# Where down's return is added in a fused attention and feed-forward kernel: one addition, one load and three subtractions change their places

## The reference, cut to what matters

```python
def attn(x):                                   # x: [16, 512, 256]
    qkv = relu(einsum('bnc,oc->bno', x, qkv_weight)).reshape(B, N, 3, 32, 8)
    q, k, v = qkv[:, :, 0], qkv[:, :, 1], qkv[:, :, 2]
    v_pad = concatenate([v, ones], axis=-1)
    vk = einsum('bnhe,bnhd->bhed', v_pad, k)
    vk_q = einsum('bhed,bnhd->bnhe', vk, q)
    att = vk_q[..., :8] / (vk_q[..., 8:] + 1e-15)
    return einsum('bnc,oc->bno', att.reshape(B, N, 256), proj_weight) + proj_bias

def ffn(x):                                    # weights are int / 127, hidden size 768
    return einsum('bsh,dh->bsd', silu(x @ wg.T) * (x @ wu.T), wd)

x1  = layernorm(x + attn(x))
out = layernorm(x1 + ffn(x1))
```

## Time and profile before

| | |
|---|---|
| time, median of 3 runs | 508.27 us (506.55 to 509.43) |
| time of the profiled execution | 506.2 us, its span 504.2 us |
| granted clock of TensorE | 0.998 over the span |
| busy: TensorE, its weight load, VectorE, ScalarE, GpSimd | 486.4, 404.4, 415.6, 255.1, 85.3 us (TensorE 96% of the span) |
| chain that ended last, by engine | TensorE 39%, DMA 24%, VectorE 22%, issue 9% |
| DMA | 85.29 MB, mean 169 GB/s |

### The profile page before, as it was taken

How to read it: one execution, slowest core, us unless ns; L and a number is a source line. 1 busy time by engine, 2 the same in 40 slices (tenths; PEclk the granted TensorE clock), 3 DMA queues, 4 the chain that set the end, 5 groups by cost and what they waited for, 6 DMA issues and landing times.

```text
span 504.2 us, 11235 instructions
## 1 busy us (share of the span) xinstructions
PE 486.4 (96%) x4292; PEld 404.4 (80%) x4292; DVE 415.6 (82%) x939; ACT 255.1 (51%) x441; POOL 85.3 (17%) x94
## 2 busy tenths in 40 slices
PE   8999999989999999999999999999999999899996
PEld 5888887868878788888887878788887887789885
DVE  5878778769879697897969879697896969799896
ACT  4667344455445444545554446444445454355553
POOL 1330110302103021020302103021030302113011
PEclk9999999999999999999999999999999999999999
DMA  8325174283763828457383763928457382632212
GB/s 327 143 76 168 42 230 148 86 282 110 249 191 133 272 94 275 141 202 229 109 273 102 253 205 111 292 96 276 140 201 221 110 280 64 223 128 72 85 42 86
DMA packets 67368, 85.29 MB, mean 169 GB/s; under 512 B 3984, under 2 KB 46736, under 8 KB 67344
## 3 DMA queue, kind: packets, MB, share of 16 engines
q1 hardware_dynamic: 67200, 84.70, 50.7%
q10 hardware_dynamic: 144, 0.26, 0.2%
HBM read 48.24 MB, written 36.18 MB: 167 GB/s over the span
## 4 chain that ended last, share of the span: by engine, by line
PE 39%; DMA 24%; DVE 22%; issue 9%; POOL 2%; ACT 2%; SPq 1%; POOLq 0%; DVEq 0%; ACTq 0%
PE abcd_ps L1050 17%; DMA down_way<-qT_first 12%; PE up_ps L1050 11%; DMA wqp_raw<-down_way 7%; PE gate_ps L1050 5%; DVE h L612 4%; PE abcd_ps L1102 3%; DVE h_lo L605 3%; DVE st L681 2%; DVE x1T_lo L605 2%; DVE xT_lo L605 2%; DMA wd_raw<-x_way 2%; DMA x_way<-wu_raw 2%; PE gate_ps L1080 2%; DVE r L698 1%
## 5 line engine op out<-in xcount | busy, mean ns | idle before, releaser
L408 ACT ACTIVATE h_hi<-h 128x512 fp32r<-128x512 f32 (+1 forms) x97 | 60.7, 627 | 92.9 <-DVE h L612 92.2
L330 POOL TENSOR_TENSOR rstd<-ve,minus_half 128x4 f32<-128x4 f32 (+2 forms) x36 | 35.2, 977 | 349.6 <-DVE ve L693 348.3
L1050 PE MATMUL up_ps<-x1T_hi,wu_hi 128*128 128x512 f32 x192 | 76.2, 397 | 9.0 <-DVE h L612 9.0
L612 DVE SCALAR_TENSOR_TENSOR h<-up_ps,silu 128x512 f32<-128x512 f32 x95 | 65.1, 685 | 16.1 <-PE up_ps L1050 13.7
L605 DVE TENSOR_TENSOR h_lo<-h,h_hi 128x512 fp32r<-128x512 f32 (+1 forms) x97 | 63.1, 676 | 17.2 <-ACT h_hi L408 16.9
L413 ACT ACTIVATE silu<-gate_ps 128x512 f32<-128x512 f32 x95 | 54.4, 585 | 42.9 <-PE gate_ps L1050 42.9
L1050 PE MATMUL gate_ps<-x1T_hi,wg_hi 128*128 128x512 f32 x192 | 74.9, 390 | 1.0 <-DVE x1T_lo L605 1.0
L1050 PE MATMUL gate_ps<-x1T_lo,wg_hi 128*128 128x512 f32 x192 | 75.2, 392 | 0.0
L1050 PE MATMUL up_ps<-x1T_lo,wu_hi 128*128 128x512 f32 x192 | 74.9, 390 | 0.0
L405 ACT ACTIVATE kv<-abcd_ps 128x512 f32<-128x512 f32 x55 | 32.9, 601 | 42.4 <-PE abcd_ps L1050 42.3
L1050 PEld LDWEIGHTS up_ps<-x1T_hi,wu_hi 128*128 128x128 f32 x192 | 36.0, 188 | 21.1 <-DVE h L612 14.0
(11 more groups left out here) (192 smaller groups left out, 1019.2 us busy)
## 6 DMA issues: line engine op xcount, KB each, us to landing
x_raw<-x_tok SPq DMA_DIRECT2D x16, 512.0 KB, 4.8
att_way<-wg_raw SPq DMA_DIRECT2D x30, 256.0 KB, 3.6
wkv_raw<-att_way SPq DMA_DIRECT2D x30, 256.0 KB, 4.6
xT_raw<-x_chan SPq DMA_DIRECT2D x14, 512.0 KB, 4.2
x_way<-wu_raw SPq DMA_DIRECT2D x28, 256.0 KB, 2.2
wd_raw<-x_way SPq DMA_DIRECT2D x28, 256.0 KB, 3.0
out<-out_sb SPq DMA_DIRECT2D x14, 512.0 KB, 3.4
x_keep<-r SPq DMA_DIRECT2D x12, 512.0 KB, 2.6
```

Source lines behind the costliest of these rows:

```text
L330: nc.gpsimd.tensor_tensor(rs[:, tiles], ve[:, tiles], minus_half[:, tiles], ALU.pow).then_inc(rs_ok, 1)
L408: nc.scalar.activation(dst, src, ACT.Copy).then_inc(ok, 1)
L612: nc.vector.scalar_tensor_tensor(out=h[:, j, :], in0=up_ps[bank_of(j)][:], scalar=HSCALE, in1=silu[:, j % 2, :], op0=ALU.mult, op1=ALU.mul ...
L1050: last = mm(dst, lhsT, rhs, start=start and n == 0, stop=stop and n == len(pairs) - 1)
```

## The change

1. On SyncE the wait for `xb_ok` and the load of `x_raw` go from ahead of down's write of half 0 to the end of `turn(i)`, behind down's read (in turn 13 behind the copy of r1).
2. On VectorE, in `ffn_half(i)`, `r2_back(i - 2, 0)` goes from ahead of `h_lo_of(i - 1, 2)` to behind `attT_lo_spread(i)`.
3. In turn 13 alone, `h_lo_of(i - 1, 3, 4, 5)` goes from the end of `attention_half` to directly behind `h_of(i - 1, 5)`, ahead of the norm and the turn of x1.

```diff
@@ sync engine, turn(i)
                 write_blocks(i + 1, att_sq, att_sq_ok, att_way, att_away)
-                sp.wait_ge(xb_ok, i + 2)
-                sp.dma_start(x_raw[:], x[i + 2]).then_inc(x_in, 16)
                 if any_i or i < NB - 3:
                     down_write(i - 1, 0)
                 read_turned(i + 1, att_way, att_away, attT_raw, attT_in)
@@
                 else:
                     sp.wait_ge(r2_ok[1], i)
                     sp.dma_start(x1[:], r1[:]).then_inc(x1_copied, 16)
+                sp.wait_ge(xb_ok, i + 2)
+                sp.dma_start(x_raw[:], x[i + 2]).then_inc(x_in, 16)
@@ vector engine, ffn_half(i)
                 h_of(i - 1, 2)
-                r2_back(i - 2, 0)
                 h_lo_of(i - 1, 2)
                 h_of(i - 1, 3)
                 attT_lo_spread(i)
+                r2_back(i - 2, 0)
                 r2_back(i - 2, 1)
                 stats_2(i - 1)
@@ vector engine, attention_half(i)
                 h_of(i - 1, 5)
+                if isinstance(i, int) and i == NB - 3:
+                    h_lo_of(i - 1, 3, 4, 5)
                 aggregated(st2, mv2, mv2_ok)
                 variance(i - 2, mv2, mv2_ok, ve2, ve2_ok)
                 x1_of(i, r1)
                 x1_blocks(i)
-                h_lo_of(i - 1, 3, 4, 5)
+                if not isinstance(i, int) or i < NB - 3:
+                    h_lo_of(i - 1, 3, 4, 5)
```

## The result

The changed kernel took 491.75 us, the median of 6 runs (491.38 to 493.56), against 507.94 us for the kernel before, the median of 6 (506.39 to 510.29). The ratio is 0.9687, 95% interval 0.9656 to 0.9719. The forecast was 493.2 us, a factor of 0.970. The profiled execution took 491.82 us with a span of 489.8 us; the forecast for it was 491.1. Two later measurements beside other kernels gave 0.9717 (0.9697 to 0.9736) and 0.9699 (0.9682 to 0.9716), so 3.0% is nearer to what the change is worth than 3.1%.

The account below looks back on a forecast made before the run. TensorE, busy 96%, was taken as the bound, held up by VectorE's addition waiting for down's return. 12.7 + 2.4 = 15.1 us off gave 491.1 for the profiled execution, 493.2 us for the median; range 489 to 500.

Parts of the forecast that it names:

- The 12 stops (12.7 us): TensorE's waits for VectorE's h in turns 2 to 13 all go: 9.0 us by column, 12.7 with surcharge.
- upper bound: Highest gain, 16.4 us (491.8): the sum plus the one stop for x1T_lo, 1.0 + 0.3 us.
- surcharge of 0.31 us: Each TensorE stop for h costs 0.31 us beyond its wait column, read from starts in two turns.
- The bound by the columns alone: Lower bound for the h stops in turns 2 to 13, trusting TensorE's wait column: 9.0 us.
- The addition's way through VectorE's order: With part 2, h of block 3 comes 1.0 us before TensorE needs it, attT_lo 0.9 us before proj.
- The load as cover only: Part 1 taken at 0 beside part 2, up to 12.7 us without it; down's halves return 0.7 to 2.3 us earlier.
- Part 3, the mis-sized term: In turn 13 TensorE's stop for h_lo goes whole: 1.4 to 2.4 us, taken as 2.4, and kept.
- 1.8 us to spare: nothing: Part 3's price in turn 13: x1T_lo ends near 438.1, TensorE wants it at 439.9, so no cost.
- B: A shorter wait, such as att's way back or late attT_lo, returns some 0.4 us per turn, 5 us: 498; chance 0.22.
- C: Most gain lost because x1's way bounds the turn: gain 3 to 8 us, 500 to 505; chance 0.06.
- D: Down's return so late that VectorE waits at the new place; only part 3 left, 506; chance 0.04.
- E: Slower: the moved load delays down's second half or the restore of x1, 518; chance 0.03.

Follow-up runs that it names:

- e1: Kernel before with part 2 alone (r2_back(i - 2, 0) behind attT_lo_spread, load of x_raw where it was): ratio 0.9745, 493.79 us.
- e4: Changed kernel without part 3 (parts 1 and 2 only): ratio 0.9727 to the kernel before, 493.29 us.
- e2: Kernel before with part 1 alone (load of x_raw behind down's read, addition at its old place): ratio 0.9735, 493.42 us.
- e5: Changed kernel without part 1 (parts 2 and 3 only): ratio 0.9762 to the kernel before, 494.21 us.
- e12: The changed kernel again, unaltered, beside others on one chip: ratio 0.9699 to the kernel before, 491.90 us.
- e9: The changed kernel once more, unaltered, on another chip: ratio 0.9717 to the kernel before, 492.45 us.
- e11: Changed kernel without part 3, measured a second time, beside the changed kernel: ratio 0.9721 to the kernel before, 493.14 us.
- e8: Changed kernel with SyncE writing att's blocks ahead of the wait for x1's way back in turn 13: ratio 0.9705 to the kernel before, 491.61 us.
- e10: Changed kernel with att's write first in turn 13 and the addition back ahead of h_lo of block 2: ratio 0.9705 to the kernel before, 492.01 us.
- e7: Changed kernel with both halves of r2_back ahead of attT_lo_spread: ratio 0.9806 to the kernel before, 497.71 us.

## Why the prediction was right

**The 12 stops (12.7 us).** Measured between proj 1 and proj 13: 13.72 us. The term for `h` was 12.7; the rest is the stop for `x1T_lo` in turn 3, which the forecast's sum didn't count as won and its upper bound did, with 1.3 us. Some 1.0 of it went: that distance is 29.83, 0.37 above the others. Whole turns bear out the surcharge of 0.31 us: against 29.46, the distances of before lost 14.19 us, where the columns add up to 10.0 and 13 surcharges of 0.31 to 4.0. The bound by the columns alone, 9.0, would have missed over a quarter.

**The addition's way through VectorE's order.** `h_lo` of block 2 starts as soon as `h_hi` is there, `h` of block 3 ends 1.0 us ahead of TensorE (256.52 against 257.52), `attT_lo` 0.93 ahead. All as forecast.

**The load as cover only.** Beside part 2 it was taken at 0 for the 12 turns, and e1 and e4, without and with it on one chip, are 0.5 us apart in their medians, within the intervals. That without part 2 it could take the stops away whole was the stated bound, and e2 shows it. Down's halves return 1.7 and 1.9 us earlier than before, counted from the turn's first gate product (6.74 and 8.61 us behind it instead of 8.43 and 10.50), inside the forecast's 0.7 to 2.3. What the step didn't see is the last turns, where the load stands in att's way (e5).

**Part 3, the mis-sized term.** 2.4 us were forecast. The whole change won 0.78 from proj 13 to proj 15 in the first profile, 0.77 in e12's, and lost 0.84 in e9's (43.01 - 43.85); without part 3, e2 has 0.58 of it and e11 0.09. The stop for `h_lo` did go whole. TensorE runs from block 2 of token tile 0 to the numerators at the pace of 0.12 us a product, beside the earlier trace rows:

```profile
414.92 0.28 PE L1054 MATMUL gate_ps<-wd_hi,h_lo 128*128 128x256 f32 x1
...
415.85 1.23 PE L1106 MATMUL abcd_ps<-vk,qT 64*64 64x72 f32 x64
```

The step that was off is the price: "1.8 us to spare: nothing" for x1's way back, 0.5 us at most for att's way, and behind them "the gain is kept". `x1T_lo` had 0.93 us to spare in the first profile (it ended at 425.30, TensorE wanted it at 426.23), and in e9 it came 0.85 late. The chain that ended last shows why the gain isn't kept. Before, it runs from VectorE's three `h_lo` into TensorE's down:

```profile
429.27 1.79 DVE h_lo L605 x3
...
431.34 0.50 PE gate_ps L1050 x2
```

In the changed kernel the same three stand on it again, ahead of x1's norm, and it goes on through x1's way:

```profile
412.37 1.80 DVE h_lo L605 x3
...
417.31 3.34 DMA x_way<-wu_raw
420.67 3.25 DMA wd_raw<-x_way
```

e1, e2, e4 and e11 have the first form, all nine profiles with part 3 the second. So part 3 took 1.8 us of VectorE's work off TensorE's path and put it on the path of x1's way. That way joins VectorE's work again, through att's way and ScalarE, or directly where att's write goes first (e8, e10). This chain is read from the profiles.

x1's write took 3.34 us and its read 3.25; the output, which waits for that return, goes out 8.1 us behind the numerators' start (415.85 to 423.94), where it was 3.1 before (431.78 to 434.90); att's write stands behind it, and ScalarE waits 1.22 us for the second half of att.

```profile
423.94 0.35 SPq L268 DMA_DIRECT2D out<-out_sb  x1
```

```profile
432.44 0.63 ACT L408 ACTIVATE attT_hi<-wkv_raw 128x512 fp32r<-128x512 f32 x1 [1.22 <-DMA wkv_raw<-att_way]
```

Of those 5.0 us, 2.4 are TensorE's own gain and 1.85 the later turn of x1, both foreseen; the remaining 0.7 are the slower transfer, which the forecast didn't have and which comes with part 3 (see the last section). Then TensorE's stop of 0.45 us for `silu`, with its surcharge, and the longer stretch from proj 14 to proj 15 (10.20 to 10.22 us with part 3 in each profile, 9.53 to 9.55 without it) take 1.4 of the 2.4 us back. TensorE comes earlier to proj 14, but ahead of proj 15 it waits for VectorE's norm of x1 by pairs, which ends the chain above, so a part of what TensorE won there had nobody to hand it to.

The total came out right although this term was too large by 1.6 us: the stop for `x1T_lo` in turn 3 gave 1.0 that the sum didn't count. That the two offset each other is luck.

**The rivals.** B's kind of loss, att's way back late, is real in turn 14 alone, not in each turn. C, D and E didn't occur: the changed kernel's turns are 29.44 to 29.49 us in all three of its profiles, but for turn 3 (29.72 to 29.94), where x1's way comes late. What C had feared, x1's way as the next limit, holds in turn 13 alone. In none of the three does VectorE's addition wait for down's return or for the restore of x1, so the load, put between those transfers, delays nothing there (rival E).

## What to carry to other kernels

An operation that waits for a transfer and that nobody needs soon belongs behind the operations that the busiest engine waits for; its place costs nothing as long as the later ones keep their slack, and the slack can be read from starts (here 0.6 us of delay were free and 1.2 were not). Two cures for one stop don't add up: price each alone, and keep the second for cover. Putting work earlier for one engine puts it ahead of everything else in its own list: the three subtractions were on the longest chain before and after. Near the end of a kernel a stop removed on one engine is worth only what the other engines' chains can follow, and a reordering that delays one transfer should be priced with all that is queued behind it.

## What the runs showed of the hardware that I had not expected

**A stop costs more than its column, and not the same everywhere:** 0.31 us more at a product with 512 columns in the middle of the turn, 0.26 at the first product of proj, with 256 columns (e7).

**Code loads and transfers meet.** In turn 13 of the changed kernel one packet of queue q8, which loads instructions (0.02 MB), falls in with x1's write. The DMA view of that stretch (the moved GB/s in 40 slices, and the queues), then x1's write in the kernel before, with no such packet in its stretch:

```profile
GB/s 0 0 0 0 156 0 0 0 20 390 293 371 390 410 293 156 20 20 0 20 0 20 0 20 39 98 351 351 371 429 410 332 195 78 0 0 0 0 0 0
...
q8 instruction: 1, 0.02, 2.0%
...
x_way<-wu_raw SPq DMA_DIRECT2D x2, 256.0 KB, 3.3
```

```profile
x_way<-wu_raw SPq DMA_DIRECT2D x2, 256.0 KB, 2.2
```

After the bulk of the write 20 GB/s trickle on for 0.9 us before the read can start. The 14 profiles leave no exception: of the writes of x1's second half from turn 2 on, the 23 that overlap such a packet of q8 took 3.05 to 4.17 us, the 159 others 2.10 to 2.51. The 23 are the write of turn 2 in all 14 profiles (that x1 is the one of turn 3, the turn with the longest distance) and that of turn 13 in the nine profiles with part 3. In the five without part 3 the write of turn 13 is over before the packet comes and took 2.32 to 2.40. So part 3 brings the two together: the write starts 1.8 us later (417.31 against 415.50 in e11), and the packet itself comes 3.3 us earlier (417.11 against 420.42); why the packet moves isn't shown. The reads of the second half took 2.82 to 3.38 us without a packet and 2.82 to 4.97 with one, so there the packet is not the whole story; the four profiles in which TensorE stopped for `x1T_lo` in turn 13 (e7 to e10) are those with part 3 whose read took 4.68 to 4.89. The Trainium skill (DMA: Bandwidth & Descriptors, "Queues, rings and completion order") says that an engine takes turns between its queues a whole packet at a time. The trickle fits one engine of the 16 that is behind for that reason, but no row here shows the engines one by one.

**The clock can fall behind a short stop.** In e4 and e1 the granted clock fell in turn 13, behind stops of 1.03 and 1.27 us for `h_lo` and one of 0.34 that follows. The windows of e4 around it (us, busy time and count of each engine, granted clock, DMA):

```profile
410.00:415.00 5.00, 4.74 (x24) 3.86 (x22) 4.85 (x20) 3.35 (x6) 2.59 (x4) 1.00 0.01 2
415.00:420.00 5.00, 3.79 (x76) 3.01 (x80) 1.92 (x4) 1.63 (x4) 0.00 (x0) 0.74 0.61 202
420.00:425.00 5.00, 5.00 (x86) 4.46 (x87) 4.09 (x9) 1.58 (x3) 2.39 (x1) 0.92 0.40 149
```

A mean of 0.74 is a part of the 5 us at 1.2 GHz instead of 2.4. The 64 products of the numerators took 2.13 us there instead of 1.16 (e11), and vk 1.06 instead of 0.70: 1.3 us. In its profile e11, the same kernel with the same stops (1.02 and 0.34 us), kept the full clock, as the kernel before did with 1.09 and 0.34. So the stop doesn't decide it alone, and what does stays open.
